# Norm scales of a macaron block made on GpSimd with one power per norm, attention banks renumbered, a transposed VectorE expansion, and a schedule that serialises a shared port

## The reference

```python
x = x + 0.5 * ffn(layernorm(x))
x = x + attn(layernorm(x))
x = x + 0.5 * ffn(layernorm(x))

def ffn(x):                                   # T = 512 tokens of a batch
    h = gamma1 * x * rsqrt(mean(x * x) + 1e-6)
    q = (h @ Wq + bq).reshape(b, t, 16, 16)
    k, v = split(((h @ Wdown + bdown) @ Wup + bup).reshape(b, t, 16, 32))
    att = softmax(einsum('bthd,btgd->bthg', q, k) / 4)      # per token, 16 heads by 16 heads
    x = x + einsum('bthg,btgd->bthd', att, v) @ Wo + bo
    h2 = gamma2 * x * rsqrt(mean(x * x) + 1e-6)
    gate = softmax(h2 @ Wg + bg)                            # 8 experts
    return x + einsum('btd,edf,bte->btf', h2, We, gate)

def attn(x):                                  # 8 heads of 32 over 512 tokens
    q, k, v = x @ Wq + bq, x @ Wk + bk, x @ Wv + bv
    return softmax(q k^T / 16) v
```

## Time and profile before

| | |
|---|---|
| median of 3 executions | 1157.16 us (1156.14 to 1158.03) |
| the profiled execution, its own time | 1162.65 us |
| its span, first to last instruction | 1160.0 us |
| around the span | 2.65 us |
| mean granted TensorE clock | 0.971 |
| busy share of the span: PE, DVE, POOL, ACT | 92%, 81%, 60%, 52% |
| DMA | 13 GB/s on average |

### The profile page before, as it was taken

One profiled execution on the slowest core, in us unless ns is written; L12 is line 12 of the kernel. 1 busy time (PEld: TensorE's weight loads), 2 busy tenths in 40 slices (PEclk: granted clock), 3 DMA queues, 4 the chain that ended last, 5 costly groups with the idle time before them and its releaser, 6 DMA issues.

```text
span 1160.0 us, 36656 instructions
## 1 busy us (share of the span) xinstructions
PE 1071.4 (92%) x15416; PEld 814.3 (70%) x15416; DVE 937.1 (81%) x1597; ACT 608.9 (52%) x1203; POOL 700.7 (60%) x627
## 2 busy tenths in 40 slices
PE   3799999999999989999999998777799999999997
PEld 3677888878787856655655655446677787888885
DVE  7979788788785379999999999987787887977853
ACT  3545345454554457767767775433453544544542
POOL 7657466366454357878878877771463654654534
PEclk9889999999999999999999998777999999999999
DMA  6210000000000000000000000000000000000000
GB/s 186 57 49 2 2 3 2 3 3 2 3 3 2 1 1 1 2 1 3 2 1 2 2 1 2 1 1 3 3 1 20 21 1 21 21 1 21 21 2 36
DMA packets 8441, 14.80 MB, mean 13 GB/s; under 512 B 2516, under 2 KB 6102, under 8 KB 8280
## 3 DMA queue, kind: packets, MB, share of 16 engines
q1 hardware_dynamic: 8280, 12.47, 3.3%
HBM read 8.28 MB, written 4.19 MB: 11 GB/s over the span
## 4 chain that ended last, share of the span: by engine, by line
PE 73%; DVE 13%; issue 4%; ACT 1%; POOL 0%; DVEq 0%; POOLq 0%; ACTq 0%
PE psum L436 47%; PE psum L602 7%; PE psum L791 5%; DVE oT L1111 5%; DVE late L1117 4%; PE psum L801 4%; PE psum L817 3%; PE psum L688 1%; PE psum L720 1%; PE psum L643 1%; PE psum L705 1%; PE psum L698 1%; PE psum L825 1%; DVE a_raw L1094 1%; DVE kvx L967 1%
## 5 line engine op out<-in xcount | busy, mean ns | idle before, releaser
L436 PE MATMUL psum<-we,h 128*128 128x512 f32 x1536 | 399.4, 403 | 0.4 <-issue 0.4
L436 PEld LDWEIGHTS psum<-we,h 128*128 128x128 f32 x1536 | 278.4, 189 | 61.1 <-issue 1.3
L1407 POOL TENSOR_TENSOR late<-late 128x512 f32<-128x512 f32 x64 | 82.6, 1291 | 204.4 <-ACT late L1250 204.4
L1111 DVE TENSOR_REDUCE oT<-psum 128x128 fp32r<-128x1024 f32 x128 | 155.4, 1216 | 33.3 <-PE psum L791 33.3
L1250 ACT ACTIVATE late<-psum,gate 128x256 f32<-128x256 f32 x256 | 107.1, 470 | 138.9 <-PE psum L436 119.3
L1300 ACT ACTIVATE kvx<-psum 128x1024 f32<-128x1024 f32 x128 | 131.1, 1024 | 78.9 <-PE psum L801 77.4
L1084 DVE SCALAR_TENSOR_TENSOR X<-psum,gate,X 128x256 f32<-128x256 f32 x256 | 122.6, 479 | 53.0 <-PE psum L436 33.0
L1445 POOL TENSOR_TENSOR kvx<-kvx,late 128x2048 f32<-128x2048 f32 x32 | 124.2, 3881 | 41.0 <-ACT late L1307 41.0
L1117 DVE TENSOR_REDUCE late<-kvx 128x256 f32<-128x2048 f32 x64 | 145.6, 2275 | 0.0
L1445 POOL TENSOR_TENSOR late<-kvx,late 128x2048 f32<-128x2048 f32 x32 | 124.4, 3888 | 34.8 <-ACT late L1307 34.8
L801 PE MATMUL psum<-oT,neg_id 128*128 128x512 f32 x256 | 96.7, 460 | 23.7 <-DVE oT L1111 23.3
(11 more groups left out here) (153 smaller groups left out, 2056.5 us busy)
## 6 DMA issues: line engine op xcount, KB each, us to landing
X<-in_L_attn_hidden_states SPq DMA_DIRECT2D x8, 512.0 KB, 5.0
out<-X SPq DMA_DIRECT2D x8, 512.0 KB, 2.9
X<-in_L_ffn_We SPq DMA_DIRECT2D x2, 1024.0 KB, 10.0
kvx<-in_L_ffn_Wq SPq DMA_DIRECT2D x1, 256.0 KB, 3.3
kvx<-in_L_ffn_Wup SPq DMA_DIRECT2D x2, 128.0 KB, 2.6
kvx<-in_L_ffn_Wo SPq DMA_DIRECT2D x1, 256.0 KB, 4.2
X<-in_L_attn_Wk SPq DMA_DIRECT2D x1, 256.0 KB, 3.0
X<-in_L_attn_Wq SPq DMA_DIRECT2D x1, 256.0 KB, 5.1
```

The costliest lines, as they stand in the source:

```text
L436: ins = e.matmul(out_ap, l, r, start=(n == 0 and not opened), stop=(n == len(terms) - 1), skip_group_check=opened)
L1111: e.tensor_reduce(mr[g // 2 % 2][:, queries(g)], heads(g), AX.X, ALU.max).then_inc(a_max, 1)
L1407: own.step(e.tensor_tensor(y[:, 0:2, :], y[:, 0:2, :], y[:, 2:4, :], ALU.add))
```

## The change

It has four parts.

1. **Norms.** `rstd`, `rms1`, `rms1_pow` and `scaled` become one step `norm` on POOL: three tensor_scalar on 128x4, one power on 128x8 (both norms' scales side by side), one tensor_tensor on 128x8. `stats` loses its last instruction. `mean` on DVE goes, and `rms2` on POOL gets a tensor_scalar in front of its power. New waits hold `norm` behind `xs` and `x1_base` of four jobs earlier, and `rms2` behind `xs2` of two jobs earlier.
2. **Banks.** The attention pairs take banks 0-1, 5-6 and 3-4, and `values` bank 2. The second feed-forward stage gets bank 3 after half 125, banks 5 and 6 after half 127, and bank 2 after the last `a_add`. The first `score` into banks 5-6 waits for both.
3. **Expansion on DVE.** The same 512 elements are walked with the 32 rows innermost and the 16 features outermost: the write steps 64 elements and the read 16 elements from one element to the next, where both went in runs before.
4. **Schedule.** The scheduler gets one more resource, "port", that every POOL step and DVE's `half` and `split_lo` hold one at a time. Some hand-written durations change.

```diff
@@ all_steps
-        put("DVE", 1950, ("stats", s), ("x1_base", s - 4, 1), ...
-        put("POOL", 1030, ("rstd", s), ("stats", s))
-        put("DVE", 550, ("rms1", s), ("rstd", s))
-        put("POOL", 1030, ("rms1_pow", s), ("rms1", s))
-        put("DVE", 500, ("scaled", s), ("rms1_pow", s))
+        put("DVE", 1800, ("stats", s), ("x1_base", s - 4, 1), ...
+        put("POOL", 2400, ("norm", s), ("stats", s))
...
-            for w, engine, ns in (("V", "DVE", 1900), ("P", "POOL", 1450), ("A", "ACT", 2150)):
+            for w, engine, ns in (("V", "DVE", 1900), ("P", "POOL", 1800), ("A", "ACT", 2150)):
...
-            put("DVE", 300, ("mean", s, w), ("square", s, own[-1]))
-            put("POOL", 1030, ("rms2", s, w), ("mean", s, w))
+            put("POOL", 1250, ("rms2", s, w), ("square", s, own[-1]))
...
+                    ("a_add", 2 * B - 1) if s == B else None)
@@ all_orders
-    kept = {("score", 1): (3, ("a_exp", 2 * units - 1)), ("score", 2): (5, ("a_exp", 2 * units - 3)),
-            ("values", 0): (6, ("a_add", 2 * B - 1))}
+    kept = {("score", 1): ((5, 6), ("a_exp", 2 * units - 1)), ("score", 2): ((3,), ("a_exp", 2 * units - 3))}
...
+    def port(p):
+
+        return steps[p][0] == "POOL" or p[0] in ("half", "split_lo")
 
     def possible(p):
-        start = max(ready[steps[p][0]][p], free[steps[p][0]])
+        start = max(ready[steps[p][0]][p], free[steps[p][0]], free["port"] if port(p) else 0)
...
+        if port(p):
+            free["port"] = end[p]
@@ macaron
-            return 2 * (g % 3)
+            return (0, 5, 3)[g % 3]
...
-                    ins = emit(kvx[c % 2][:, rows, :, t4, :].rearrange("p r w d -> p (r w) d"),
-                               kvc[c % 3][:, rows, :, :].rearrange("p r w d -> p (r w) d"), mask4[:, t4:t4 + 1])
+                    order = "p r w d -> p d (r w)" if who == "V" else "p r w d -> p (r w) d"
+                    ins = emit(kvx[c % 2][:, rows, :, t4, :].rearrange(order),
+                               kvc[c % 3][:, rows, :, :].rearrange(order), mask4[:, t4:t4 + 1])
@@ dve_program
-                    own.step(ins)
-                    e.wait_ge(own.sem, own.n)
-                    e.tensor_scalar(r[:, 3, :], m[:, :, 1], LN_EPS, None, ALU.add).then_inc(s_stat, 1)
-                elif name == "rms1":
...
-                elif name == "scaled":
...
+                    ins.then_inc(s_stat, 1)
@@ pool_program
+                if name == "norm":
...
+                    if k >= 4:
+                        e.wait_ge(s_xs, 2 * (k - 3))
+                        e.wait_ge(s_x1p, 2 * (k - 3))
                     e.wait_ge(s_stat, k + 1)
-                    e.tensor_tensor(r[:, 0, :], r[:, 3, :], half_neg[:, 0:NT], ALU.pow).then_inc(s_rstd, 1)
+                    own.step(e.tensor_scalar(r[:, 0, :], m[:, :, 1], 1.0, LN_EPS, ALU.mult, ALU.add))
+                    own.step(e.tensor_scalar(r[:, 1, :], m[:, :, 1], 1.0 + RMS_EPS, LN_EPS * RMS_EPS, ALU.mult, ALU.add))
+                    own.step(e.tensor_scalar(nm[:, 2, :], m[:, :, 0], -1.0, 1.0, ALU.mult, ALU.mult))
+                    e.wait_ge(own.sem, own.n)
+                    both = r[:, :, :].rearrange("p a i -> p (a i)")
+                    own.step(e.tensor_tensor(both, both, half_neg[:, 0:2 * NT], ALU.pow))
+                    e.wait_ge(own.sem, own.n)
+                    e.tensor_tensor(nm[:, 0:2, :], r[:, :, :], nm[:, 2, :].unsqueeze(1).to_broadcast([P, 2, NT]),
+                                    ALU.mult).then_inc(s_rs, 1)
```

More of the change, by code:

```diff
@@ L155, in all_steps @@
             put("DVE", 680, ("oT_lo", s, p), ("oT_hi", s, p))
-            put("POOL", 2450, ("x1_base", s, p), ("scaled", s), ("half", s - 1, before), ("xs2", s - 1, before),
+            put("POOL", 2450, ("x1_base", s, p), ("norm", s), ("half", s - 1, before), ("xs2", s - 1, before),
                 ("score", 2 * units) if s >= B else None)
@@ L299, in banks, with empty @@
         if p[0] in WIDE:
-            return (3,)
+            return ((3,),)
         if p[0] in RING:
-            return (7,) if p[0] in ("a_hT", "qk", "v") and p[1] else (5, 6, 7)
+            return ((7,),) if p[0] in ("a_hT", "qk", "v") and p[1] else ((5,), (6,), (7,))
         return ()
-    def empty(bank):
-        p = holder[bank]
-        return 0 if p is None else end.get(kept[p][1] if p in kept else (TAKEN[p[0]][-1], *p[1:]), never)
+    def empty(choice):
+        last = [holder[bank] for bank in choice if holder[bank]]
+        return max((end.get(kept[p][1] if p in kept else (TAKEN[p[0]][-1], *p[1:]), never) for p in last), default=0)
+    def port(p):
+        return steps[p][0] == "POOL" or p[0] in ("half", "split_lo")
     def possible(p):
-        start = max(ready[steps[p][0]][p], free[steps[p][0]])
+        start = max(ready[steps[p][0]][p], free[steps[p][0]], free["port"] if port(p) else 0)
         return max(start, min((empty(b) for b in banks(p)), default=-hop) + hop)
@@ L460, in macaron @@
         mv = [sb(f"mv{n}", [P, NT, 2]) for n in range(4)]
-        rs = [sb(f"rs{n}", [P, 4, NT]) for n in range(4)]
+        rs = [sb(f"rs{n}", [P, 2, NT]) for n in range(4)]
         xs = sb("xs", [P, NT, D])
@@ L588, in freed_by @@
                 return a_exp, 2 * units if n == 1 else 2 * units - 2
-            return a_add, 2 * B
-        before = {p: freed_by(q) for p, q in held.items() if q}
+            raise KeyError(piece)
+        before = {p: [freed_by(q) for q in earlier] for p, earlier in held.items()}
         def windows(e, left, right, w):
@@ L1399, in pool_program @@
                 elif name == "rms2":
-                    own_t = span(tiles_in(k, piece[2]))
-                    e.wait_ge(s_ms, done(k, piece[2]))
+                    tiles = tiles_in(k, piece[2])
+                    own_t = span(tiles)
+                    if k >= 2:
+                        e.wait_ge(s_xs2, done(k - 2))
+                    e.wait_ge(s_sq, 2 * k + tiles[-1] // 2 + 1)
+                    own.step(e.tensor_scalar(rms[k % 2][:, own_t], ssq[k % 2][:, own_t], 1.0 / D, RMS_EPS, ALU.mult, ALU.add))
+                    e.wait_ge(own.sem, own.n)
                     e.tensor_tensor(rms[k % 2][:, own_t], rms[k % 2][:, own_t], half_neg[:, own_t], ALU.pow).then_inc(s_rms2, 1)
```

72 lines of the change are left out of this document (26 added, 46 removed).

## The result

The changed kernel takes **1172.54 us** (median of 4 runs, 1170.35 to 1177.94), the kernel before 1157.6 in the same session: ratio 1.0137, 95% interval 1.0099 to 1.0174. It is slower by 15 us where the prediction said 18 faster. The profiled execution shown here has 1170.35 us, its span is 1168.3.

What follows compares the result with a forecast made beforehand. PE was taken to bound both feed-forward stages and DVE attention's last units, with start and seam loose. Terms -1.0 - 4.3 - 8.2 - 3.0 + 2.6 - 4.2 = -18.1 took 1157.16 to 1139 us; range for 8 in 10, 1126 to 1160.

Steps and rivals of the forecast that it cites:

- Norms, in steady jobs: Steady feed-forward jobs: norm work moved to POOL stays covered by PE's work; -1.0 us for inputs that come sooner.
- The expansion on DVE: Each chunk: 0.69 us per strided instruction, alternation with POOL gone, three take what they take now; 0 us.
- rival 2: DVE's expansion keeps both ports and pays for its stride, POOL's grows likewise; +5 us, 1144 us, chance 0.15.
- The start: First jobs: job 0's norm chain wins 1.4 us, job 1's 2.89 us wait for its xs goes; -4.3 us.
- Attention's last units: Attention's end, bound by DVE: small norm instructions no longer wait behind POOL's normalise; -8.2 us.
- First expansion: Seam behind attention: DVE's three instructions come before the last normalise, 1.9 us instead of 4.92; -3.0 us.
- POOL (+2.6): Seam: POOL does job 9's norm in front of the last normalise, delaying what stands behind; +2.6 us.
- clock (-4.2): Seam: PE gets work in the hole ahead of its half-clock stretch, winning half of 8.4 us; -4.2 us.
- Rival 1: Seam gives little, as kv, chunk 17 and all experts still follow the last normalise; 7 us lost, 1146 us, chance 0.23.
- Banks and port: Second stage's banks look like an exchange, the port only changes the order; 0 us, -2 to +3 in the range.
- rival 3: Strided expansion at 1.1 us an instruction uses up the room in steady jobs and seams; 34 us, 1173 us, chance 0.12.
- what would show it: Trace signs listed beforehand: waits gone at attention's end, first PE transpose near 10 us, short half-clock stretches, DVE's expansion at 0.69.

Runs made afterwards that it cites:

- with slack: Changed kernel, planner believing scores ready 2.5 us and attend 1.5 us later than computed: 1163.1 us; with DVE's old expansion layout too, 1147.9 us.
- the shifts: 64 or 128 waits added before TensorE's first instruction: 1168.7 and 1174.5 us in the changed kernel; 128 in the kernel before, 1155.6 us.

## Why the prediction was wrong

Step by step, by its own terms:

- **Norms, in steady jobs (-1.0, between 0 and -4.8): the step that failed first.** It called the work covered by PE's 98% and bounded it by PE's gaps, thus on the side of a gain only. The cover was one in the mean. What a steady job has to spare is the slack in front of its four runs of products, 2.1 us behind the second expansion, and a run stops for code long before that reaches zero: of the runs with the block's end in their last 80 records 97 of 108 stopped below 1.5 us of slack. In the change that slack fell to 0.75 us, and the steady jobs, with all four parts together, took 29 us more where this term had 1 less. Alone the norms cost 10 us, although in that trace the seam won 13.
- **The expansion on DVE (0): the step that failed most.** DVE's side was nearly right: 0.62 us at best and 0.72 at the median, three in 1.86 in second chunks; the mean grew from 790 to 871 ns, 6 us of DVE in all. The other side was not priced in the sum. The expectation that the alternation goes is refuted by POOL's expansions (a pair takes 1.36 us alone and 2.26 beside DVE's at 1039). That is rival 2's mechanism, and it was costed at +5 because 2.1 us of room seemed to cover the steady jobs. It costs 15.2 us with slack and 15 in the kernel before, and only 2 in the change itself. On the mode the Trainium skill ("VectorE: DVE Perf Modes", on what the auto-detection checks) agrees with these rows: the stride did not end what DVE and POOL do to each other. Its granule rule ("Vector Engine (DVE) Microarchitecture Reference", section 5.2) has the direction right and the size wrong here: the estimate from its figure was 1.36 us an instruction, the fastest took 0.62.
- **The start (-4.3): mis-sized.** The first transpose came 1.7 us sooner, the first expert of job 1 by 1.7 us. From the last aggregate to the first xs it takes 3.1 us (6.19 to 9.27, forecast 2.8), because the power of eight columns takes 1.65 us for an estimated 1.47, and job 1's share was hardly seen.
- **Attention's last units (-8.2): right on DVE.** From half 110's maximum to the last `a_total` it is 50.7 us for 60.8, 10 us sooner for a forecast of 5; L904 and L909 are gone. The last `normalise`, which POOL now does behind chunk 16 and job 9's norm, ends only 3.6 us sooner by the same measure (65.1 us for 68.8).
- **First expansion (-3.0), POOL (+2.6), clock (-4.2): right in sum, low in size.** Last units and seam together won 20.6 us for a forecast of 12.8. 0.50 of the clock now stands at 761.8 to 768.6 and 799.3 to 802.7 alone, where the earlier trace rows had 20.5 us in one piece and 0.80 ahead of it. Rival 1 is out: job 8's experts begin 34.0 us behind the last `values`, 42.9 before.
- **Banks and port (0, -2 to +3).** The banks are worth nothing with slack (0.6 us) and cost 7 us alone; why those fall in the last jobs of the second stage is not settled. The port costs nothing alone, and taking it out of the change costs 10 us; which of its orders does that was not tried apart.
- **The range** (1126 to 1160) missed: of the cases only rival 3 lay past it. Its 1173 is the measured time by luck, on another road: it needed 1.1 us an instruction, and the median is 0.72.

Of "what would show it", the gone waits, the early transpose, the clock and DVE's 0.69 (median 0.72) came true; of the signs of "wrong", POOL's longer pairs and the longer steady jobs. What the sum lacked was a row on what PE does when its operands come 1 us later. The trace before had a hint that was read past, the group of L602 with its 9.6 us on "issue".

## What to carry to other kernels

"PE is 98% busy, so work beside it is free" holds only as long as each run of short products finds its operands early. Read the time between the last operand and the run's start, not the busy share, and treat a change that shortens it as a cost, here from some 2.5 us downward. Where gaps are put down to "issue", count the engine's records: gaps that always stand at one place of a block of 256 are waits for code. Putting other products in front of the run helped where operands came late (9.5 us) and cost 5 us where they did not. And test the parts of a change with more than one list: the norms here were a loss of 10 us in one list and a win of 13 in another. Where a planner makes all lists anew for every edit, a few microseconds either way can belong to the new order and not to the edit; no experiment here held the lists fixed except those on the layout and the shifts.

## What the runs showed of the hardware

- TensorE stops for its own instructions: 266 of 266 gaps inside runs stand at the same place of a 256-record block and end 2.16 to 2.96 us after a 16 KB transfer begins, and waits added at the start of the stream move them to other products. What sets a transfer off was not found. It starts late where PE's operands come late: of the steady runs with the block's end in their last 80 records, it began 1.03 us or more behind the last operand in 97 of the 108 with less than 1.5 us of slack, and these 97 stopped; above 2.5 us of slack 34 of 150 stopped.
- A back-to-back series of DVE's strided expansions made POOL wait for its whole length in four steady chunks (a pair of 1.09 us took 2.53), while a series with POOL's turns in between costs both sides (2.48 us for DVE's three, 2.26 for POOL's pair at 1038 us).
- GpSimd's power grows with its width faster than from 2 to 4 columns: 783 ns, 1011 ns, 1650 ns for 2, 4 and 8 columns, 0.114 us and then 0.160 us a column.
